# The scalars of a Householder step: one VectorE operation on a pair for pivot and divisor, one GpSimd multiply-add for the new column's seed part

## The reference

```python
deg = A.sum(axis=0) + A.sum(axis=1) - diagonal(A)
L_norm = d_inv_sqrt[:, None] * (diag(deg) - A) * d_inv_sqrt[None, :]
_, U = eigh(L_norm)
agg = einsum('mn,bnd->bmd', U.T, layernorm_relu(x))
x = x + einsum('nm,bmd->bnd', U, relu(agg @ W1 + b1) @ W2 + b2)
# second layer: relu(adj @ (h Wg0 + bg0)), again with Wg1, then four short LSTMs
```

## Time and profile before

| | |
|---|---|
| median of three runs | 1609.99 us |
| the profiled execution, and its span | 1610.8 us, 1609.0 us |
| the 255 steps | about 21 to 787 us |
| sweeps, vectors, layers | 787 to 1609 us |
| busy in 21 to 787 us | PE 644.8, DVE 661.6, POOL 345.7, ACT 223.9 us |
| TensorE's granted clock in that stretch | 1.00 |

### The profile page before, as it was taken

The page is one execution under the profiler, slowest core; times in us unless marked ns, Lnnn a source line. Parts: engine busy times, 40 slices in busy tenths (PEclk is TensorE's granted clock), DMA queues, the critical chain, the costliest instruction groups (busy, mean ns, idle before and its releaser), DMA issues.

```text
span 1609.0 us, 25379 instructions
## 1 busy us (share of the span) xinstructions
PE 1273.3 (79%) x6001; PEld 1065.8 (66%) x6001; DVE 1257.9 (78%) x6154; ACT 609.6 (38%) x2116; POOL 396.6 (25%) x2138
## 2 busy tenths in 40 slices
PE   6999999999996667777445444473999989999997
PEld 5777888888874555555334332262778779999997
DVE  6898988888888888888899999998682255556555
ACT  1222222222233434322121321250234577778765
POOL 5333333343445555555300000002000010000000
PEclk9999999999999999999988676676999999999999
DMA  7000000000000000000000000000000000000011
GB/s 171 1 1 1 1 2 1 1 2 1 1 1 2 1 1 1 1 1 1 1 0 1 0 1 0 1 1 1 1 1 1 0 1 1 1 1 27 1 28 53
DMA packets 23404, 12.66 MB, mean 8 GB/s; under 512 B 5075, under 2 KB 22230, under 8 KB 23254
## 3 DMA queue, kind: packets, MB, share of 16 engines
q1 hardware_dynamic: 23254, 11.03, 2.8%
HBM read 6.83 MB, written 4.19 MB: 7 GB/s over the span
## 4 chain that ended last, share of the span: by engine, by line
DVE 47%; PE 36%; issue 8%; POOL 6%; ACT 2%; DVEq 1%; DMA 0%; POOLq 0%
PE bank L822 10%; PE bank L824 6%; PE bank L831 5%; DVE A L1039 4%; DVE RC L1127 4%; DVE O L1135 3%; PE bank L666 3%; PE bank L669 3%; DVE pa L1123 3%; DVE O L1021 3%; DVE O L1131 3%; DVE junk L991 2%; DVE zc L1033 2%; DVE wk L1025 2%; DVE NG L1006 2%
## 5 line engine op out<-in xcount | busy, mean ns | idle before, releaser
L611 ACT ACTIVATE H<-bank,gate_b 128x128 f32<-128x128 f32 (+2 forms) x624 | 213.0, 440 | 75.2 <-PE bank L824 72.3
L669 PEld LDWEIGHTS bank<-O 128*128 128x128 f32 x764 | 201.5, 344 | 0.0
L822 PE MATMUL bank<-O,WlT 128*128 128x256 f32 (+1 forms) x896 | 189.6, 325 | 7.8 <-DVE O L1403 5.6
L678 PE MATMUL bank<-O,y 128*128 128x2 f32 x510 | 142.3, 349 | 65.4 <-DVE y L991 60.1
L474 ACT ACTIVATE ncp<-pc,RC 128x2 f32<-128x2 f32 (+1 forms) x254 | 74.9, 295 | 292.6 <-DVE RC L1012 292.6
L666 PE MATMUL bank<-ident,O 128*128 128x128 f32 x382 | 148.2, 457 | 47.5 <-DVE O L1021 35.5
L678 PEld LDWEIGHTS bank<-O,y 128*128 128x128 f32 x510 | 128.2, 312 | 77.5 <-issue 72.3
L669 PE MATMUL bank<-O 128*128 128x1 f32 x764 | 162.8, 305 | 0.0
L822 PEld LDWEIGHTS bank<-O,WlT 128*128 128x128 f32 x896 | 147.8, 190 | 21.5 <-ACT H L611 9.2
L686 PE MATMUL bank<-ident,pc 128*128 128x128 f32 x381 | 147.7, 457 | 5.5 <-DVE pc L1010 2.2
L666 PEld LDWEIGHTS bank<-ident,O 128*128 128x128 f32 x382 | 60.1, 198 | 135.3 <-DVE O L1021 135.3
(11 more groups left out here) (399 smaller groups left out, 3124.6 us busy)
## 6 DMA issues: line engine op xcount, KB each, us to landing
X<-in_x SPq DMA_DIRECT2D x2, 2048.0 KB, 14.5
out<-X SPq DMA_DIRECT2D x32, 128.0 KB, 1.9
adj_sb<-in_adj SPq DMA_DIRECT2D x1, 256.0 KB, 3.0
W1s<-in_L_gnn_W SPq DMA_DIRECT2D x1, 64.0 KB, 9.6
W2s<-in_L_gnn_W SPq DMA_DIRECT2D x1, 64.0 KB, 2.6
Wg0s<-in_L_gnn_Wg SPq DMA_DIRECT2D x1, 64.0 KB, 2.4
Wg1s<-in_L_gnn_Wg SPq DMA_DIRECT2D x1, 64.0 KB, 3.6
Wl<-in_L_gnn_Wih SPq DMA_DIRECT2D x1, 0.5 KB, 6.6
```

Of the source, the lines that this page charges most:

```text
L611: ins = a(gates[:, q, i, 0:n], gate_at(p, q, i), fn, bias=gate_b[:, p - 1, i:i + 1])
L669: ins = mm(bank[0][:, 0:1], R[:, b, k, 0:1].to_broadcast([P, P]), R[:, b, k, 0:1], start=(b == bl[0]), stop=(b == 1))
L678: ins = mm(sb_[:, 0:2], y[:, 1:2].to_broadcast([P, P]), R[:, 1, k, :], start=True, stop=(k >= P - 1))
L822: last = mm(gate_at(p, q, i), WlT[:, 0, p - 1, i, :], window(c, p, t, part), start=True, stop=(t == 0))
```

## The change

`half` becomes a pair. Its second element is half * x0, one more VectorE operation, placed behind the multiply-and-sum (its semaphore is `hx_ready`). TensorE writes sigma to column 1 of bank 0, and column 0 is set to zero once, before the steps, so that bank 0 holds the pair (0, sigma). One operation then forms both scalars: the pair `NG[:, k, :]` = (half, half * x0) * root - (0, sigma). L1002 and L1006 are gone, and with them the semaphore `g1_ready`. What the reciprocal waited for goes with it; `pc` waits for the pair; the wait for `xm` moves from the old L1006 to `cx`. On GpSimd `tm` is ym * 1/pb + seed in one tensor_scalar with two columns as its scalars, one for each row block, and `sy` and `yb` are gone.

```diff
-        root = sb("root", [P, 1]); half = sb("half", [P, 1]);
+        root = sb("root", [P, 1]); half = sb("half", [P, 2])
...
-                    pool.wait_ge(S["pb_ready"], k + 1)
-                    g.tensor_tensor(sy[:, bs], tmp[:, bs, c0 + 1], pb.to_broadcast([P, w]), ALU.mult).then_inc(S["sy_ready"], 1)
-                    pool.wait_ge(S["sy_ready"], k + 1)
-                    g.tensor_tensor(yb[:, bs], ym[:, bs], sy[:, bs], ALU.add).then_inc(S["yb_ready"], 1)
-                    pool.wait_ge(S["yb_ready"], k + 1)
+                    pool.wait_ge(S["ym_ready"], k + 1)
                     pool.wait_ge(S["c_ready"], k + 1)
-                    g.tensor_tensor(tm[:, bs], yb[:, bs], RC[:, k, 0:1].to_broadcast([P, w]), ALU.mult).then_inc(S["t_ready"], 1)
+                    for b in range(b0, 2):
+                        ins = g.tensor_scalar(tm[:, b:b + 1], ym[:, b:b + 1], RC[:, k, 0:1], tmp[:, b, c0 + 1:c0 + 2], ALU.mult, ALU.add)
+                    ins.then_inc(S["t_ready"], 1)
...
+            v.memset(bank[0][:, 0:1], 0.0)
...
+                dve.wait_ge(S["half_ready"], k + 1)
+                tt(half[:, 1:2], half[:, 0:1], x0, ALU.mult).then_inc(S["hx_ready"], 1)
                 if b0 == 0:
                     dve.wait_ge(S["y_part"], k + 1)
                     dve.wait_ge(S["y01_ready"], k + 1)
...
-                dve.wait_ge(S["half_ready"], k + 1)
+                dve.wait_ge(S["hx_ready"], k + 1)
                 dve.wait_ge(S["root_ready"], k + 1)
-                tt(pb, root[:], half[:], ALU.mult).then_inc(S["pb_ready"], 1)
-                if not last:
-                    dve.wait_ge(S["xm_ready"], k + 1)
+                stt(out=NG[:, k, :], in0=half[:], scalar=root[:], in1=zs, op0=ALU.mult, op1=ALU.subtract).then_inc(S["pb_ready"], 1)
                 dve.wait_ge(S["pb_ready"], k + 1)
-                stt(out=NG[:, k, 1:2], in0=pb, scalar=x0, in1=sigma, op0=ALU.mult, op1=ALU.subtract).then_inc(S["g1_ready"], 1)
...
-                dve.wait_ge(S["g1_ready"], k + 1)
                 v.reciprocal(RC[:, k, :], NG[:, k, :]).then_inc(S["c_ready"], 1)
                 if last:
                     break
+                dve.wait_ge(S["xm_ready"], k + 1)
                 dve.wait_ge(S["c_ready"], k + 1)
                 tt(cx[:, bs], xm[:, bs], nc_.to_broadcast([P, w]), ALU.mult).then_inc(S["cx_ready"], 1)
```

More of the change, by code:

```diff
@@ L112, in gnn_kernel @@
         y = sb("y", [P, 2]); ym = sb("ym", [P, 2]); tm = sb("tm", [P, 2]); pc = sb("pc", [P, 2]); ncp = sb("ncp", [P, 2])
-        xm = sb("xm", [P, 2]); cx = sb("cx", [P, 2]); zc = sb("zc", [P, 2]); sy = sb("sy", [P, 2]); yb = sb("yb", [P, 2]); vt = sb("vt", [P, 2])
+        xm = sb("xm", [P, 2]); cx = sb("cx", [P, 2]); zc = sb("zc", [P, 2]); vt = sb("vt", [P, 2])
         gqn = sb("gqn", [P, 1]); kc = sb("kc", [P, 1]); wk = sb("wk", [P, 1])
@@ L179, in gnn_kernel @@
             lt_rdy adjT_rdy adjT_cp wlt_ps wlt_cp biases
-            x_ready xrow_ready sig_ready root_ready g1_ready y_part y01_ready y0_ready y1_ready half_ready pb_ready p_ready c_ready
-            xm_ready ym_ready vt_ready v_ready kc_ready ncp_ready sy_ready yb_ready t_ready s_ready prow_ready cx_ready gq_ready w_ready z_ready add0 add1 upd0 upd1 s_hist d0_ready seed_rdy half_upd
+            x_ready xrow_ready sig_ready root_ready y_part y01_ready y0_ready y1_ready half_ready hx_ready pb_ready p_ready c_ready
+            xm_ready ym_ready vt_ready v_ready kc_ready ncp_ready t_ready s_ready prow_ready cx_ready gq_ready w_ready z_ready add0 add1 upd0 upd1 s_hist d0_ready seed_rdy half_upd
             ln_sum ln_mean ln_var ln_root ln_rstd ln_shift ln_norm
@@ L469, in _ @@
                 act.wait_ge(S["sig_ready"], k + 1)
-                a(root[:], bank[0][:, 0:1], ACT.Sqrt, scale=4.0).then_inc(S["root_ready"], 1)
+                a(root[:], bank[0][:, 1:2], ACT.Sqrt, scale=4.0).then_inc(S["root_ready"], 1)
                 if not last:
@@ L668, in _ @@
                 for b in bl:
-                    ins = mm(bank[0][:, 0:1], R[:, b, k, 0:1].to_broadcast([P, P]), R[:, b, k, 0:1], start=(b == bl[0]), stop=(b == 1))
+                    ins = mm(bank[0][:, 1:2], R[:, b, k, 0:1].to_broadcast([P, P]), R[:, b, k, 0:1], start=(b == bl[0]), stop=(b == 1))
                 ins.then_inc(S["sig_ready"], 1)
@@ L982, in _ @@
                 x0, s_, y0_ = xb[:, c0:c0 + 1], sb_[:, 0:1], sb_[:, 1:2]
-                sigma = bank[0][:, 0:1]
+                zs = bank[0][:, 0:2]
                 pb, prn, nc_ = NG[:, k, 0:1], RC[:, k, 0:1], RC[:, k, 1:2]
                 dve.wait_ge(S["xrow_ready"], k + 1)
-                ts(half[:], x0, 0.0, 0.5, ALU.is_lt, ALU.subtract).then_inc(S["half_ready"], 1)
+                ts(half[:, 0:1], x0, 0.0, 0.5, ALU.is_lt, ALU.subtract).then_inc(S["half_ready"], 1)
                 for b in reversed(bl):
```

## The result

| | us, median (runs) | ratio to the kernel before, 95% |
|---|---|---|
| before | 1610.26 (1609.72 to 1612.92) | 1 |
| after | 1643.08 (1642.85 to 1643.39) | 1.0195 [1.0180, 1.0211] |

The change makes the kernel 2% slower, by 33 us where 36 were forecast. (The row of the kernel before has one run more than the median given ahead of the prediction.) The page of the kernel after: busy time by engine, the chain that ended last by engine and line, and the groups of the new `tm` and of the new column.

What follows compares the result with a forecast made beforehand. Step length was taken to bound the kernel, set by waits over wk, TensorE with GpSimd's tm, or VectorE and the root. Losses 5 + 20 + 11 = 36 us; 1610.8 + 36 - 0.8 = 1646 us, range 1601 to 1668.

Steps and rivals of the forecast that it cites:

- Pair operation: VectorE, one operation forming both scalars: RC 0.52 becomes 0.38 behind its start, 0.14 us won in a wide step.
- half * x0 hidden in wide steps: VectorE's added operation, 0.15 to 0.16 us, between read and y; late wide steps hide it in y's idle 0.25.
- GpSimd's d: Duration of one new tensor_scalar for tm on GpSimd: taken as 0.39 us, forecast band 0.36 to 0.43.
- rival 3: GpSimd's tensor_scalar lasts 0.25 to 0.36 us, VectorE's gain is eaten in part: 1607 to 1635 us; chance 12%.
- The 0.30 from reciprocal to `tm`: GpSimd's tm starts 0.31 us behind RC in an early narrow step of the kernel before; 0.30 was taken.
- First 40 wide steps: Earliest wide steps, bound over wk, which comes 0.13 us later in each: 5 us lost.
- Other 86: Remaining wide steps, bound by the chain of waits over TensorE: 0.23 us lost in each, 20 us.
- the circle over `wk`: Chain of waits through wk, 0.30 us behind the new column; taken to bound the first 40 wide steps.
- Narrow steps: Steps with one row block: 0.14 us lost over the first 40, 6 us; 5 more over some 50, then none.
- Rival 1: GpSimd's tensor_scalar as cheap as what it replaces, 0.19 to 0.25 us: 1603 us, 1594 with cx's second wait free; 29%.
- Rival 4: VectorE's pc held until GpSimd's ym ends, 0.17 us later: 22 us on top of the forecast, 1668 us; chance 4%.

Runs made afterwards that it cites:

- the best kernel here: Kernel before with pair operation and tm on VectorE in wide steps only, and late waits written first, except wk's in narrow steps: 1574.33 us, ratio 0.9761.

## Why the prediction was right, and where its sum was lucky

- *Pair operation*: `pc` 0.38 and `RC` 0.52 behind `y`, `cx` 0.26 behind `RC`, 0.19 from read to pair: each as worked out.
- *half * x0 hidden in wide steps*: right; `y` follows the read by 0.12 in early ones, before and after.
- *GpSimd's d*: taken at 0.39, measured 0.34. That is outside the forecast's own band (0.36 to 0.43) and in rival 3's (0.25 to 0.36), whose price was 1607 to 1635. The time came out at the forecast since two terms were too small: `tm` starts 0.33 or 0.34 behind `RC` (taken 0.30), and the second tensor_scalar 0.32 behind the first where 0.34 less the prediction's 0.04 or 0.05 would be 0.30 or 0.29. In a wide step the sum is 0.52 + 0.33 + 0.66 + 0.03 = 1.54 for 1.58, in a narrow one 1.10 for 1.105. The mechanism was right; that the errors in its sizes cancelled was luck.
- *The 0.30 from reciprocal to `tm`* was read from a row that doesn't show it. In the early narrow step of the kernel before, `yb` (the row below) ends at 503.00 and `tm` starts 0.08 later: it waits for `yb`, not for the reciprocal. The number was all the same right for a product (0.30) and 0.04 short for a tensor_scalar (0.34), by the experiments.

```profile
502.81 0.19 POOL L320 TENSOR_TENSOR yb<-ym,sy 128x1 f32<-128x1 f32 x1
```

- *First 40 wide steps*: 5 forecast, 3.0 measured. *Other 86*: 20 and 16.5. The loss is 0.10 a step between steps 40 and 50, 0.20 between 70 and 80 and 0.26 between 100 and 120. The prediction let the circle over `wk`, which loses less, end at step 40. In the run with `wk`'s waits turned, an earlier `wk` still shortens steps 50 to 60 by 0.07 each and 70 to 80 by 0.04, and from 90 on by nothing: that circle fades out between 60 and 90.
- *Narrow steps*: 11 forecast, 13.0 measured. Pair to column was right; what was missed is the column operation's 0.26, which keeps the root 0.05 later, so that the last 47 steps lost 2.1 where none was forecast.
- *Rival 1* was priced well: 1603 against 1603.7 measured with a cheap operation, 1594 against 1596.4 with `cx`'s wait moved as well. What decided between it and the forecast was the price of one kind of operation that the trace of before did not hold.
- *Rival 4*: `pc` starts at 409.09, in `ym`'s 409.07 to 409.27, and takes its 0.22. The Trainium skill, "SBUF — State Buffer", section "Who interferes with whom", states an exclusive lock for this pair of operations. At this size it doesn't show here; a stretch of the column by 0.043 in narrow steps does.
- The Trainium skill, "GPSIMD Engine Reference", section 3.1, has tensor_tensor slowed by its second input. For tiles of one or two columns this is turned round: 0.19 with two tensor inputs, 0.34 with one and two column scalars. The cost sits in the scalars, which the section's account by elements does not contain.

## What to carry to other kernels

Fewer instructions on an idle engine are no gain in themselves: ask which result each one starts from. Only the last of the old chain's operations needed the reciprocal: in a wide step the reciprocal is done at 402.61, when `ym` (402.15 to 402.35) and `sy` are done and `yb` is under way.

```profile
402.57 0.20 POOL L320 TENSOR_TENSOR yb<-ym,sy 128x2 f32<-128x2 f32 x1
```

In the new chain everything but `ym` stands behind the reciprocal. Where a loop changes its bound as it goes (here the width of the step), measure each form and each order of waits in both regimes; the best kernel here uses a different one in each.

## What the runs showed of the hardware

- A GpSimd operation at 128x1 takes 0.19 as tensor_tensor, as copy and as tensor_scalar with two numbers, 0.21 as tensor_scalar with one number, 0.29 with one column scalar, 0.34 with two; at 128x2 tensor_tensor and the form with two column scalars take the same.
- Behind the 0.16 reciprocal of VectorE that it waits for, a GpSimd tensor_tensor starts at 0.30, a tensor_scalar with column scalars at 0.34.
- Of two waits on a VectorE instruction, the one written second costs 0.07 when it is met last, the one written first no more than a single wait (0.03 to 0.04): from end to start 0.11 became 0.04, and `wk` 0.30 behind the column became 0.23.
- Two VectorE operations that don't wait for each other start 0.08 apart if the first is a tensor_tensor of 0.16, 0.13 apart if it is a scalar_tensor_tensor of 0.22.
- In narrow steps a GpSimd operation that began 0.06 or 0.07 into VectorE's column operation stretched it from 0.22 to 0.26; one that began before it did not. In wide steps the same distance came with 0.22 or with 0.26.
